# Routing weights of a mixture-of-experts block: transposed by TensorE, or by their transfer to device memory

## The chip, the cores and the metric

The kernel runs on one core of a Trainium2 chip. The metric is device time in microseconds; before the change it is 2189.81 us (median of three runs, 2189.57 to 2190.14).

## The reference

Input `x` is 16 batches x 512 tokens x 128 features, all float32. A first stage adds gated attention (16 heads of 64, causal). The second stage, where the change is, computes for each token:

```python
h = layernorm(x) * (1 + cb) + sb                      # cb, sb, gb per batch
logits = h @ Wr + br                                  # 8 experts
masked = where(logits >= second_largest, logits, -inf)
weights = softmax(masked)                             # two of eight are non-zero
hid = gelu(h @ W1[e] + b1[e])                         # 128 -> 512, each expert
y = sum_e (hid @ W2[e] + b2[e]) * weights[:, e]       # 512 -> 128
x = x + gb * y
```

All eight experts are computed for all tokens.

## The kernel before, in words

Each engine runs its own instruction list, written out by hand, and the lists meet at semaphores. There are two stages, one after the other: attention for all 16 batches (until about 1420 us of the span), then the experts for all 16 batches. Only the second stage is touched.

In the second stage the 512 tokens of a batch lie along the free axis and the features (or hidden units) on the 128 partitions. The stage runs batch by batch (`b`, the first and last written out, the 14 between in a loop), and in each batch over the experts `e` = 0 to 7. A product of high precision is made of three products of rounded operands (high x high, low x high, high x low). The order in one expert step is:

- TensorE: `first_layer(b, e)`, 4 chunks of 128 hidden units, 12 matmuls (L869 to L871); then `second_layer(b, e-1)`, 12 matmuls (L882 to L884) into one of two PSUM banks. TensorE is one expert ahead of itself, so that the activation of `e` lies beside the second layer of `e-1`. Extra work: at e = 1 `sum_T(b-1)` (four transposes, L891), at e = 3 `norm_T` (L845), at e = 4 `router_logits` (L851), at e = 6 `weights_T` (L858), all but the first for batch b+1.
- ScalarE (ACT): four GELU evacuations (L1005) and the rounded high part of chunks 0 and 1 (L1013). Extra: at e = 4 `h_evac`, at e = 5 the exponential, at e = 7 `weights_out` (L985) and `round_h` (L978), at e = 1 `gate_sum` (L992).
- VectorE (DVE): `rest_chunk` for four chunks: the low part (L1124), for chunks 2 and 3 also the high part (L1122); then `weigh_expert(b, e-1)` (L1137). Extra: statistics at e = 1 (L1066, L1069), `finish` (L1146), normalised rows at e = 2 (L1074), `choose` at e = 4 (L1084 to L1091), `weights` at e = 5 (L1096 to L1103), `rest_h` at e = 7 (L1079, in front of chunk 1).
- GpSimd (POOL): `add_expert` (L943) adds each weighted expert to `acc`.
- SP issues the transfers: `store(b-1)`, then `lay_weights(b+1)`.

The weights' way before the change: DVE writes `w_now` as [token, tile, expert] in a buffer of 128 columns per tile whose other columns POOL cleared once (L955). TensorE transposes its four 128x128 tiles into PSUM bank 6 (L858), ACT copies the 8 rows of 512 to `w_T` (L985), SP stores them in device memory as rows of 2 KB (L1198) and, when they have landed, loads each expert's row back to all 128 partitions (`w_rows`, L1204). The row of expert `e` may be overwritten once the batch before has been weighed with it (`y_weighted`). `weigh_expert` computes (y + b2) * weight with `w_rows[:, e, :]` read contiguously.

TensorE waits for `hid_lo_ok` of each chunk before the second layer, for `r_lo` (from `rest_h`) before the first layer of a new batch, and for the weighing two experts back before it reuses a PSUM bank.

Of the kernel before, what the change touches and what calls it, by code (L numbers as in the profile page):

```python
# [7 lines left out]
ALU = mybir.AluOpType  # L8
ACT = mybir.ActivationFunctionType
AX = mybir.AxisListType  # L10
ds = bass.ds
# [27 lines left out]
def adaln_moe_kernel(nc, resid, W_Q, W_K, W_V, W_out, b_out, W1, b1, W2, b2, Wr, br, c_in, wmod, out):  # L39
# [10 lines left out]
    with ExitStack() as ctx:  # L50
# [3 lines left out]
        def sem(name):  # L54
            return ctx.enter_context(nc.semaphore(name))
# [709 lines left out]
        with ExitStack() as pb:  # L765
            def sbb(name, shape, dt=F32):
                return sb(name, shape, dt, pb)
# [17 lines left out]
            shifted = sbb("shifted", [P, NT, E])  # L785
            expd = sbb("expd", [P, NT, E])
            kept = sbb("kept", [P, NT, E])
            w_now = sbb("w_now", [P, NT, P])
            w_sum = sbb("w_sum", [P, NT])
            w_rsum = sbb("w_rsum", [P, NT])  # L790
            w_T = sbb("w_T", [E, S])


            w_rows = sbb("w_rows", [P, E, S])
# [4 lines left out]
            y_result = sbb("y_result", [P, NT, D])  # L799
            y_banks = [banks[:, 4, :], banks[:, 5, :]]  # L800

            hT_bank, wT_bank, out_bank = banks[:, 6, :], banks[:, 6, :], banks[:, 6, :]
            logit_bank = banks[:, 7, 0:NT * E]

            def tile_of(x, b, t):
# [11 lines left out]
            def expert(b, e):  # L817
# [1 line left out]
                return E * b + e  # L819

            load_w = [[sem(f"load_w{layer}_{e}") for e in range(E)] for layer in (1, 2)]
            w_hi_ok, w_split_ok, w_now_clear = sem("w_hi_ok"), sem("w_split_ok"), sem("w_now_clear")
            r_stat, r_mv, r_eps, r_rstd, r_xn = (sem(f"r_{n}") for n in ("stat", "mv", "eps", "rstd", "xn"))
            r_T_ps, r_full, r_hi, r_lo = (sem(f"r_{n}") for n in ("T_ps", "full", "hi", "lo"))
            r_logit_ps, r_shift, r_exp, r_w, r_wT_ps, r_wT = (
                sem(f"r_{n}") for n in ("logit_ps", "shift", "exp", "w", "wT_ps", "wT"))
            w_written = sem("w_written")
            w_laid = [sem(f"w_laid_{e}") for e in range(E)]
            r_chain = sem("r_chain")
# [9 lines left out]
            with nc.Block() as block:  # L839
                @block.tensor  # L840
                def _(pe):
# [6 lines left out]
                    def router_logits(b):  # L848
# [2 lines left out]
                            mm = pe.matmul(logit_bank[:, t * E:(t + 1) * E], hf[:, t * P:(t + 1) * P],  # L851
                                           wr_sb[:, :], start=True, stop=True)
                        mm.then_inc(r_logit_ps, 1)

                    def weights_T(b):
                        pe.wait_ge(r_w, b + 1)
                        for t in range(NT):
                            mm = pe.transpose(wT_bank[:, t * P:(t + 1) * P], w_now[:, t, :], ident[:, :])  # L858
                        mm.then_inc(r_wT_ps, 1)

                    def first_layer(b, e, begin):
                        if e == 0:
# [32 lines left out]
                    def body(b, first, last):  # L895
                        for e in range(E):
                            if first:
                                pe.wait_ge(w_split_ok, e + 1)
                            first_layer(b, e, first and e == 0)
                            if e == 0 and first:  # L900
                                weights_T(0)
                            if first and e > 0:
                                pe.wait_ge(w_split_ok, E + e)
                            if e > 0:
                                second_layer(b, e - 1, first and e < 3)
                            elif not first:
                                second_layer(b - 1, E - 1, False)
                            if e == 1 and not first:
                                sum_T(b - 1)
                            if not last and e == 3:  # L910
                                norm_T(b + 1)
                            if not last and e == 4:
                                router_logits(b + 1)
                            if not last and e == 6:
                                weights_T(b + 1)
                            if first and e == E - 1:
                                pe.wait_ge(w_split_ok, 2 * E)

# [6 lines left out]
                @block.gpsimd  # L925
                def _(pool):
                    def inv_std(b):

                        wait_alone(pool, r_mv, NT * b + NT)
                        pool.tensor_scalar(var_eps[:, :], meanvar[:, :, 1], EPS, 1.0, ALU.add, ALU.mult).then_inc(r_eps, 1)  # L930
                        pool.wait_ge(r_eps, b + 1)
                        pool.tensor_tensor(rstd[:, :], var_eps[:, :], neg_half[:, :], ALU.pow).then_inc(r_rstd, 1)

                    def summed(b, e):

                        return (E - 1) * b + e

                    def add_expert(b, e):
                        wait_alone(pool, y_weighted, expert(b, e) + 1)
                        if e > 1:  # L940

                            wait_alone(pool, y_summed, summed(b, e - 1))
                        pool.tensor_tensor(acc[:, :], acc[:, :], y_w[:, :], ALU.add).then_inc(y_summed, 1)  # L943

                    def body(b, first, last):
                        if not first:
                            add_expert(b - 1, E - 1)
                        if not last:
                            inv_std(b + 1)
                        for e in range(1, E - 1):  # L950
                            add_expert(b, e)

                    inv_std(0)

                    pool.memset(w_now[:, :, :], 0.0).then_inc(w_now_clear, 1)  # L955
                    batches(pool, body)
                    add_expert(B - 1, E - 1)

                @block.scalar
                def _(act):  # L960
# [12 lines left out]
                    def round_h(b):  # L973
# [2 lines left out]

                            act.wait_ge(hid_ps, HC * expert(b, 0))
                        act.activation(h2_hi[:, :], hf[:, :], ACT.Copy).then_inc(r_hi, 1)  # L978

                    def weights_out(b):  # L980
                        act.wait_ge(r_wT_ps, b + 1)
                        if not isinstance(b, int) or b > 0:

                            act.wait_ge(w_written, 16 * b)
                        act.activation(w_T[:, :], wT_bank[0:E, :], ACT.Copy).then_inc(r_wT, 1)  # L985

                    def gate_sum(b):
                        act.wait_ge(y_summed, (E - 1) * (b + 1))
# [26 lines left out]
                    def body(b, first, last):  # L1015
                        for e in range(E):
                            young = first and e < 2
                            if first and e == 1:
                                for other in range(HC):
                                    round_w(2, other)  # L1020

                                act.wait_ge(w_split_ok, E + HC)
                            if first and HC <= e + 2 < E:
                                round_w(2, e + 2)
                            hidden_chunk(b, e, 0, young)
                            if e == 0 and first:
                                weights_out(0)
                            if e == 4 and not last:
                                h_evac(b + 1)
                            if e == 7 and not last:  # L1030
                                weights_out(b + 1)
                            hidden_chunk(b, e, 1, young)
                            round_chunk(b, e, 0, young)
                            hidden_chunk(b, e, 2, young)
                            if e == 7 and not last:
                                round_h(b + 1)
                            round_chunk(b, e, 1, young)
                            hidden_chunk(b, e, 3, young)
                            if e == 1 and not first:
                                gate_sum(b - 1)  # L1040
                            if e == 5 and not last:
                                logit_exp(b + 1)
# [10 lines left out]
                def _(dve):  # L1053
# [40 lines left out]
                    def weights(b):  # L1094
# [2 lines left out]
                        link(b, dve.tensor_reduce(w_sum[:, :], kept[:, :, :], AX.X, ALU.add))  # L1097
                        link(b, dve.reciprocal(w_rsum[:, :], w_sum[:, :]))
                        rsum = w_rsum[:, :].unsqueeze(2).broadcast_to([P, NT, E])
                        if isinstance(b, int) and b == 0:  # L1100

                            dve.wait_ge(w_now_clear, 1)
                        dve.tensor_tensor(w_now[:, :, 0:E], kept[:, :, :], rsum, ALU.mult).then_inc(r_w, 1)  # L1103
                        assert links[0] == CHAIN

                    def split_w(i, layer, e):
# [5 lines left out]
                    def rest_chunk(b, e, c, young):  # L1112
# [3 lines left out]
                        else:  # L1116
# [7 lines left out]
                        dve.tensor_tensor(hid_lo[:, e % 2, c, :], full, hi.bitcast(F32), ALU.subtract)\  # L1124
                            .then_inc(hid_lo_ok, 1)

                    def weigh_expert(b, e, begin):

                        dve.wait_ge(y_ps, expert(b, e) + 1)
# [4 lines left out]
                        if e > 1:  # L1134

                            dve.wait_ge(y_summed, (E - 1) * b + e - 1)
                        dve.scalar_tensor_tensor(out=acc[:, :] if e == 0 else y_w[:, :], in0=y_banks[e % 2],  # L1137
                                                 scalar=b2_cols[:, e:e + 1], in1=w_rows[:, e, :],
                                                 op0=ALU.add, op1=ALU.mult).then_inc(y_weighted, 1)

                    def finish(b, begin):
# [44 lines left out]
                def _(sp):  # L1186
# [7 lines left out]
                                     W2[e].rearrange("(c p) d -> p c d", p=P)).then_inc(load_w[1][e], 16)  # L1194

                    def lay_weights(b, first):
                        sp.wait_ge(r_wT, b + 1)
                        sp.dma_start(w_kept[ds(b, 1)].rearrange("b e s -> e (b s)"), w_T[:, :]).then_inc(w_written, 16)  # L1198
                        sp.wait_ge(w_written, 16 * (b + 1))
                        for e in range(E):  # L1200
                            if not first:
# [45 lines left out]
```

## Time and profile before

| | |
|---|---|
| median of three runs | 2189.81 us |
| the profiled execution | 2190.27 us, its span 2188.5 us |
| TensorE (PE) matmuls | 2047.3 us busy, 94% of the span |
| VectorE (DVE) | 1700.8 us, 78% |
| ScalarE (ACT) | 1531.4 us, 70% |
| GpSimd (POOL) | 722.2 us, 33% |
| granted TensorE clock | 0.994 of full speed |

"Busy" is the time in which an engine has an instruction under way; matmuls overlap one another, so the start-to-start distance of matmuls is the better clock of TensorE. Names such as `banks` are all PSUM banks; `b_cols` stands for `b1_cols` or `b2_cols`, `w_hi` for the high part of either weight.

### The profile page before, as it was taken

Reading aid. Unit: us, or ns where it says so; the run is one execution under the profiler, and the core shown is the slowest. Engines: PE = TensorE matmul, PEld = TensorE weight load, DVE = VectorE, ACT = ScalarE, POOL = GpSimd, SP = SyncE. Lnnn points to the kernel's source line nnn. Section 1 sums busy time; section 2 is a strip of 40 time slices with the busy share of each in tenths; the row PEclk is TensorE's granted clock in tenths of the full one; section 3 lists DMA queues with packets and bytes.
Section 4 is the critical chain, followed back from the end, with each engine's and each line's share of the span. In section 5 each row is a group of like instructions: output and inputs, shape, how many; then the busy total and the mean of one; then the engine's idle time right before and its main releaser. Section 6 shows DMA issues by size and latency. Waiting matters only on the chain. (4 is left out here: it accounts for less than half of the span.)

```text
span 2188.5 us, 45861 instructions
## 1 busy us (share of the span) xinstructions
PE 2047.3 (94%) x12751; PEld 1550.8 (71%) x12751; DVE 1700.8 (78%) x4517; ACT 1531.4 (70%) x3749; POOL 722.2 (33%) x1215
## 2 busy tenths in 40 slices
PE   5999999999999999999999999879999999999998
PEld 3676666666666666667666667568888888888887
DVE  5877767777777677777777777579999888898887
ACT  4777667667677676676677767567776777676775
POOL 2334334333333333333343434212222222222222
PEclk9999999999999999999999999989999999999999
DMA  3000000000000000000000000031211112111111
GB/s 109 16 1 1 0 1 1 0 0 1 0 1 0 1 1 0 1 1 0 1 0 0 1 0 1 1 116 47 75 50 47 43 43 69 56 48 43 43 47 45
DMA packets 41996, 49.99 MB, mean 23 GB/s; under 512 B 3176, under 2 KB 23712, under 8 KB 41888
## 3 DMA queue, kind: packets, MB, share of 16 engines
q1 hardware_dynamic: 41632, 48.41, 7.0%
q0 software_dynamic: 256, 0.53, 0.1%
q14 instruction: 88, 0.72, 0.1%
q8 instruction: 20, 0.33, 0.1%
HBM read 44.47 MB, written 4.46 MB: 22 GB/s over the span
## 5 line engine op out<-in xcount | busy, mean ns | idle before, releaser
L340 POOL TENSOR_SCALAR probs<-probs,rdenom 128x512 f32<-128x512 f32 (+3 forms) x1024 | 522.4, 532 | 840.6 <-DVE rdenom L694 840.6
L564 ACT ACTIVATE probs<-probs,neg_max 128x512 f32<-128x512 f32 (+3 forms) x1024 | 562.8, 553 | 287.2 <-DVE neg_max L685 287.2
L685 DVE CUSTOM_DVE_ANT_0 probs<-banks,mask_w 128x512 f32<-128x512 f32 (+3 forms) x1024 | 441.0, 485 | 66.7 <-PE banks L398 53.5
L1005 ACT ACTIVATE hidden<-banks,b_cols 128x512 f32<-128x512 f32 x512 | 348.4, 685 | 198.5 <-PE banks L871 172.9
L1124 DVE TENSOR_TENSOR hid_lo<-hidden,hid_hi 128x512 fp32r<-128x512 f32 x512 | 386.7, 763 | 67.5 <-ACT hid_hi L1013 55.2
L427 PE MATMUL banks<-ident,probs 128*128 128x128 f32 x2560 | 392.2, 280 | 46.4 <-DVE z_lo L698 34.0
L427 PEld LDWEIGHTS banks<-ident,probs 128*128 128x128 f32 x2560 | 289.7, 141 | 154.0 <-DVE probs_T L674 50.7
L943 POOL TENSOR_TENSOR acc<-acc,y_w 128x512 f32<-128x512 f32 x112 | 155.1, 1385 | 489.5 <-DVE y_w L1137 489.5
L439 PE MATMUL banks<-probs_T,v_sb 128*64 128x512 f32 (+3 forms) x2048 | 303.9, 439 | 1.6 <-DVE probs_T L674 1.6
L674 DVE COPY probs_T<-banks 128x512 f32<-128x512 f32 x384 | 261.7, 681 | 55.4 <-PE banks L427 54.6
L439 PEld LDWEIGHTS banks<-probs_T,v_sb 128*64 128x64 f32 x2048 | 136.0, 137 | 152.4 <-issue 124.2
L398 PE MATMUL banks<-k_hi,q_hi 64*128 64x512 f32 (+3 forms) x1024 | 189.1, 361 | 46.1 <-DVE k_lo L662 31.9
L698 DVE TENSOR_TENSOR z_lo<-banks,z_hi 128x512 fp32r<-128x512 f32 x128 | 88.5, 692 | 160.1 <-ACT z_hi L576 160.1
L869 PE MATMUL banks<-h_hi,w_hi 128*128 128x512 f32 x512 | 207.2, 405 | 3.8 <-DVE w_lo L1110 2.6
L882 PE MATMUL banks<-hid_hi,w_hi 128*128 128x512 f32 x512 | 199.6, 390 | 1.9 <-DVE w_lo L1110 1.9
L871 PE MATMUL banks<-h_lo,w_hi 128*128 128x512 f32 x512 | 200.9, 392 | 0.0
L870 PE MATMUL banks<-h_hi,w_lo 128*128 128x512 f32 x512 | 200.6, 392 | 0.0
L884 PE MATMUL banks<-hid_lo,w_hi 128*128 128x512 f32 x512 | 199.6, 390 | 0.0
L883 PE MATMUL banks<-hid_hi,w_lo 128*128 128x512 f32 x512 | 199.4, 390 | 0.0
L564 ACT ACTIVATION_READ_ACCUMULATOR probs<-probs,neg_max 128x1 f32 x1024 | 194.6, 190 | 0.0
L398 PEld LDWEIGHTS banks<-k_hi,q_hi 64*128 64x128 f32 x1024 | 99.1, 184 | 105.3 <-issue 81.8
L398 PE MATMUL banks<-k_hi,q_lo 64*128 64x512 f32 (+3 forms) x1024 | 168.7, 320 | 0.0
(138 smaller groups left out, 3506.2 us busy)
## 6 DMA issues: line engine op xcount, KB each, us to landing
w_rows<-w_kept SPq DMA_DIRECT2D x128, 256.0 KB, 3.9
x_all<-in_L_attn_resid_dram SPq DMA_DIRECT2D x16, 256.0 KB, 2.6
out_dram<-y_result SPq DMA_DIRECT2D x16, 256.0 KB, 2.3
w_raw<-in_L_ffn_W_dram SPq DMA_DIRECT2D x12, 256.0 KB, 4.0
hidden<-in_L_ffn_W_dram SPq DMA_DIRECT2D x4, 256.0 KB, 6.3
v_sb<-in_L_attn_W_Q_dram SPq DMA_DIRECT2D x1, 512.0 KB, 6.0
v_sb<-in_L_attn_W_K_dram SPq DMA_DIRECT2D x1, 512.0 KB, 8.1
v_sb<-in_L_attn_W_V_dram SPq DMA_DIRECT2D x1, 512.0 KB, 11.2
```

The lines of the kernel that those rows point to most:

```text
L340: pool.tensor_scalar(part, part, rdenom[:, p % 2, 4 * h + r:4 * h + r + 1], 1.0, ALU.mult, ALU.mult)\
L398: mm = pe.matmul(s_banks[S_BANK[u] + h][:, at:at + n], q[own, p % 2, rows], k[own, p % 2, 0:n], start=start, stop=stop)
L427: mm = pe.transpose(T_BANK[u][:, at:at + P], probs[:, p % 2, h, src:src + P], ident[:, :])
L439: mm = pe.matmul(z_bank[h * DH:(h + 1) * DH, c * P:S], v_sb[:, c, hc:hc + DH], probs_T[:, h, KEY_AT[c]:KEY_AT[c] + n], start=(c == 0), sto ...
L564: act.activation(part, part, ACT.Exp, bias=neg_max[:, p % 2, col:col + 1], scale=-1.0, accum_out=denom[:, p % 2, col:col + 1]).then_inc(p_ ...
L674: dve.tensor_copy(dst, src).then_inc(t_dve, 1)
L685: dve.tensor_tensor_reduce(out=probs[:, p % 2, h, at:at + n], in0=s_banks[S_BANK[u] + h][:, col:col + n], in1=mask_w[:, 512 - n:512], scal ...
L869: pe.matmul(banks[:, c, :], w1_hi[:, e, cols], h2_hi[:, :], start=True, stop=False)
L870: pe.matmul(banks[:, c, :], w1_lo[:, e, cols], h2_hi[:, :], start=False, stop=False)
L871: pe.matmul(banks[:, c, :], w1_hi[:, e, cols], h2_lo[:, :], start=False, stop=True)\
L1005: act.activation(hidden[:, e % 2, c, :], banks[:, c, :], ACT.Gelu, bias=b1_cols[:, e * HC + c:e * HC + c + 1]).then_inc(hid, 1)
L1124: dve.tensor_tensor(hid_lo[:, e % 2, c, :], full, hi.bitcast(F32), ALU.subtract)\
```

## The change

`w_now` becomes [token, expert, tile] (32 values per token). SP stores it as it is: for each token `p` of a tile and each expert the four tiles' values lie side by side, 16 bytes, and go to position `4 p` of the expert's row in device memory. There are 128 x 8 = 1024 such runs in the 16 KB. The TensorE transposes, the ACT copy, `w_T` and POOL's clearing go. The rows that come back are in the order (token, tile), and `weigh_expert` reads them with a step of four values (16 bytes) so that they meet y in the order (tile, token). DVE now waits for the store of the batch before (`w_written`) ahead of writing `w_now`.

```diff
-            w_now = sbb("w_now", [P, NT, P])
+            w_now = sbb("w_now", [P, E, NT])
-            w_T = sbb("w_T", [E, S])
@@ TensorE
-                    def weights_T(b):
-                        pe.wait_ge(r_w, b + 1)
-                        for t in range(NT):
-                            mm = pe.transpose(wT_bank[:, t * P:(t + 1) * P], w_now[:, t, :], ident[:, :])
-                        mm.then_inc(r_wT_ps, 1)
-                            if e == 0 and first:
-                                weights_T(0)
-                            if not last and e == 6:
-                                weights_T(b + 1)
@@ POOL
-                    pool.memset(w_now[:, :, :], 0.0).then_inc(w_now_clear, 1)
@@ ACT
-                    def weights_out(b): ...
-                        act.activation(w_T[:, :], wT_bank[0:E, :], ACT.Copy).then_inc(r_wT, 1)
-                            if e == 0 and first:
-                                weights_out(0)
-                            if e == 7 and not last:
-                                weights_out(b + 1)
@@ DVE
-                        if isinstance(b, int) and b == 0:
-                            dve.wait_ge(w_now_clear, 1)
-                        dve.tensor_tensor(w_now[:, :, 0:E], kept[:, :, :], rsum, ALU.mult).then_inc(r_w, 1)
+                        if not isinstance(b, int) or b > 0:
+                            wait_alone(dve, w_written, 16 * b)
+                        dve.tensor_tensor(w_now[:, :, :].rearrange("p e t -> p t e"), kept[:, :, :], rsum, ALU.mult).then_inc(r_w, 1)
+                    def by_tile(a):
+                        return a[:, :].rearrange("d (t p) -> d t p", t=NT)
-                        dve.scalar_tensor_tensor(out=acc[:, :] if e == 0 else y_w[:, :], in0=y_banks[e % 2],
-                                                 scalar=b2_cols[:, e:e + 1], in1=w_rows[:, e, :],
+                        dve.scalar_tensor_tensor(out=by_tile(acc if e == 0 else y_w),
+                                                 in0=y_banks[e % 2].rearrange("d (t p) -> d t p", t=NT),
+                                                 scalar=b2_cols[:, e:e + 1],
+                                                 in1=w_rows[:, e, :].rearrange("d (p t) -> d t p", t=NT),
                                                  op0=ALU.add, op1=ALU.mult).then_inc(y_weighted, 1)
@@ SP
-                        sp.wait_ge(r_wT, b + 1)
-                        sp.dma_start(w_kept[ds(b, 1)].rearrange("b e s -> e (b s)"), w_T[:, :]).then_inc(w_written, 16)
+                        sp.wait_ge(r_w, b + 1)
+                            sp.dma_start(w_kept[ds(b, 1)].rearrange("b e (p t) -> p (b e) t", t=NT), w_now[:, :, :])\
+                                .then_inc(w_written, 16)
```

## Rows read from the trace of the kernel before

**Rows 1.** Busy time by stretch: length, PE, PEld, DVE, ACT, POOL, clock, DMA share, GB/s.
```profile
1701.70:1747.95 46.25, 46.14 (x214) 38.07 (x213) 41.35 (x82) 33.35 (x56) 10.92 (x9) 1.00 0.16 51
```
**Rows 2.** Timeline of PE in one batch: start, length, operation, count.
```profile
1705.69 0.39 PE L869 MATMUL banks<-h_hi,w_hi 128*128 128x512 f32 x1
...
1711.14 0.60 PE L858 MATMUL banks<-ident,w_now 128*128 128x128 f32 x4
1711.50 0.48 PE L869 MATMUL banks<-h_hi,w_hi 128*128 128x512 f32 x1
...
1714.33 0.39 PE L882 MATMUL banks<-hid_hi,w_hi 128*128 128x512 f32 x1
...
1717.05 0.40 PE L869 MATMUL banks<-h_hi,w_hi 128*128 128x512 f32 x1
```
**Rows 3.** Groups by line, 1520 to 2110 us: busy us, mean ns, idle before.
```profile
L1122 DVE CAST hid_hi<-hidden 128x512 fp32r<-128x512 f32 x205 | 85.9, 419 | 0.0
L1137 DVE SCALAR_TENSOR_TENSOR y_w<-banks,b_cols,w_rows 128x512 f32<-128x512 f32 x89 | 66.3, 745 | 0.0
L985 ACT ACTIVATE w_T<-banks 8x512 f32<-8x512 f32 x13 | 7.4, 571 | 0.0
```
**Rows 4.** Groups by line, 60 to 180 us (attention), one operation at two widths.
```profile
L685 DVE CUSTOM_DVE_ANT_0 probs<-banks,mask_w 128x512 f32<-128x512 f32 x24 | 15.6, 687 | 3.8 <-PE banks L398 3.7
L685 DVE CUSTOM_DVE_ANT_0 probs<-banks,mask_w 128x128 f32<-128x128 f32 x24 | 6.8, 284 | 0.0
```
**Rows 5.** Timeline of DVE in one batch; in brackets idle before, and releaser.
```profile
1708.56 0.84 DVE L1103 TENSOR_TENSOR w_now<-kept,w_rsum 128x32 f32<-128x32 f32 x1
...
1710.45 0.69 DVE L1124 TENSOR_TENSOR hid_lo<-hidden,hid_hi 128x512 fp32r<-128x512 f32 x1 [0.40 <-ACT hid_hi L1013]
...
1713.18 0.75 DVE L1137 SCALAR_TENSOR_TENSOR y_w<-banks,b_cols,w_rows 128x512 f32<-128x512 f32 x1
1714.76 1.35 DVE L1124 TENSOR_TENSOR hid_lo<-hidden,hid_hi 128x512 fp32r<-128x512 f32 x1 [0.83 <-ACT hid_hi L1013]
1716.03 0.68 DVE L1079 TENSOR_TENSOR h_lo<-hf,h_hi 128x512 fp32r<-128x512 f32 x1
...
1721.04 1.36 DVE L1124 TENSOR_TENSOR hid_lo<-hidden,hid_hi 128x512 fp32r<-128x512 f32 x1 [0.34 <-ACT hid_hi L1013]
...
1725.38 0.69 DVE L1124 TENSOR_TENSOR hid_lo<-hidden,hid_hi 128x512 fp32r<-128x512 f32 x1 [0.19 <-ACT hid_hi L1013]
1726.48 1.29 DVE L1124 TENSOR_TENSOR hid_lo<-hidden,hid_hi 128x512 fp32r<-128x512 f32 x1 [0.41 <-ACT hid_hi L1013]
...
1729.82 0.74 DVE L1137 SCALAR_TENSOR_TENSOR acc<-banks,b_cols,w_rows 128x512 f32<-128x512 f32 x1
...
1743.45 1.79 DVE L1124 TENSOR_TENSOR hid_lo<-hidden,hid_hi 128x512 fp32r<-128x512 f32 x2 [1.05 <-ACT hid_hi L1013]
```
**Rows 6.** Timeline of POOL in the same batch.
```profile
1708.05 1.29 POOL L943 TENSOR_TENSOR acc<-acc,y_w 128x512 f32<-128x512 f32 x1 [4.70 <-DVE y_w L1137]
1714.26 1.29 POOL L943 TENSOR_TENSOR acc<-acc,y_w 128x512 f32<-128x512 f32 x1 [4.92 <-DVE y_w L1137]
1720.36 1.48 POOL L943 TENSOR_TENSOR acc<-acc,y_w 128x512 f32<-128x512 f32 x1 [4.81 <-DVE y_w L1137]
1725.46 1.76 POOL L943 TENSOR_TENSOR acc<-acc,y_w 128x512 f32<-128x512 f32 x1 [3.61 <-DVE y_w L1137]
...
1742.67 1.29 POOL L943 TENSOR_TENSOR acc<-acc,y_w 128x512 f32<-128x512 f32 x1 [4.87 <-DVE y_w L1137]
```
**Rows 7.** Timeline of SP's DMA issues in the same batch.
```profile
1713.81 0.32 SPq L1198 DMA_DIRECT2D w_kept<-w_T  x1
1715.47 10.22 SPq L1204 DMA_DIRECT2D w_rows<-w_kept  x8
```
**Rows 8.** The page on DMA: a queue's packets, MB, share of 16 engines; issues, KB, us to landing.
```profile
q1 hardware_dynamic: 41632, 48.41, 7.0%
...
w_rows<-w_kept SPq DMA_DIRECT2D x128, 256.0 KB, 3.9
```

More of the change, by code:

```diff
@@ L800, in adaln_moe_kernel @@
             y_banks = [banks[:, 4, :], banks[:, 5, :]]
-            hT_bank, wT_bank, out_bank = banks[:, 6, :], banks[:, 6, :], banks[:, 6, :]
+            hT_bank, out_bank = banks[:, 6, :], banks[:, 6, :]
             logit_bank = banks[:, 7, 0:NT * E]
@@ L821, in adaln_moe_kernel @@
             load_w = [[sem(f"load_w{layer}_{e}") for e in range(E)] for layer in (1, 2)]
-            w_hi_ok, w_split_ok, w_now_clear = sem("w_hi_ok"), sem("w_split_ok"), sem("w_now_clear")
+            w_hi_ok, w_split_ok = sem("w_hi_ok"), sem("w_split_ok")
             r_stat, r_mv, r_eps, r_rstd, r_xn = (sem(f"r_{n}") for n in ("stat", "mv", "eps", "rstd", "xn"))
             r_T_ps, r_full, r_hi, r_lo = (sem(f"r_{n}") for n in ("T_ps", "full", "hi", "lo"))
-            r_logit_ps, r_shift, r_exp, r_w, r_wT_ps, r_wT = (
-                sem(f"r_{n}") for n in ("logit_ps", "shift", "exp", "w", "wT_ps", "wT"))
+            r_logit_ps, r_shift, r_exp, r_w = (
+                sem(f"r_{n}") for n in ("logit_ps", "shift", "exp", "w"))
             w_written = sem("w_written")
@@ L978, in round_h @@
                         act.activation(h2_hi[:, :], hf[:, :], ACT.Copy).then_inc(r_hi, 1)
[L980 to L984, printed above, removed]
-                        act.activation(w_T[:, :], wT_bank[0:E, :], ACT.Copy).then_inc(r_wT, 1)
                     def gate_sum(b):
@@ L1196, in lay_weights @@
                     def lay_weights(b, first):
-                        sp.wait_ge(r_wT, b + 1)
-                        sp.dma_start(w_kept[ds(b, 1)].rearrange("b e s -> e (b s)"), w_T[:, :]).then_inc(w_written, 16)
+                        sp.wait_ge(r_w, b + 1)
+                        with nc.allow_non_contiguous_dma("expert rows of the routing weights"):
+                            sp.dma_start(w_kept[ds(b, 1)].rearrange("b e (p t) -> p (b e) t", t=NT), w_now[:, :, :])\
+                                .then_inc(w_written, 16)
                         sp.wait_ge(w_written, 16 * (b + 1))
```

## The prediction

> **What bounds the kernel now.** I read the busy time by stretch first. One period of the expert stage is 46.25 us; TensorE is busy in 46.14 of them, DVE in 41.35, ACT in 33.35, POOL in 10.92 [rows 1]. So TensorE sets the pace, and the reader should see how near DVE is behind it. TensorE's timeline gives the unit: from 1705.69 to 1711.14 lie 24 matmul starts, 0.227 us each [rows 2]. 192 of them are 43.6 us; transposes, logits and a short wait make up the rest.
>
> DVE's 41.35 us hide something. The timelines of DVE and POOL, laid beside each other, show that the two exclude each other when DVE reads two operands from the local memory: the product written to hid_lo lasts 0.69 us at 1710.45, but 1.35 at 1714.76, 1.36 at 1721.04 and 1.29 at 1726.48, each time until POOL's addition is through [rows 5, 6]. The other way about, POOL's addition takes 1.29 us where DVE leaves it alone and 1.76 at 1725.46, where a DVE product had just begun. Even the small write of w_now lasts 0.84 us, up to the end of the addition that began at 1708.05 [rows 5, 6]. POOL takes part of DVE's time, then, about 1.15 us per addition (1.76 less the 0.61 that the product at 1725.38 still had to run).
>
> **How much can DVE take on?** Its idle pieces, all with ACT as releaser, are 0.40, 0.83, 0.34, 0.19, 0.41 and 1.05 us [rows 5]. A DVE that is late would not wait for ACT, but it would still have to let POOL through. The 0.34 and 0.41 lie inside POOL's turns (1720.36 with 1.48, 1725.46 with 1.76 [rows 6]) and can't be had. Of the 0.83 some 0.55 can, since the addition of 1714.26 would start after the product in place of before it; of the 1.05 some 0.36, by the same working with the addition of 1742.67 [rows 6]. With 0.40 and 0.19 that is 1.5 us. DVE needs 46.25 - 1.5 = 44.75 us per period, against TensorE's 46.25.
>
> **The change, part by part.**
>
> *TensorE's four transposes go.* From 1711.14 to 1714.33 stand the transposes and 12 matmuls: 3.19 us, less 12 x 0.227 = 2.72, is 0.47 us [rows 2]. TensorE's period falls to 45.78. There are 15 such places in running batches: 7.0 us if nothing else is late. What is late next is `rest_h`, which ends at 1716.03 + 0.68 = 1716.71 [rows 5], while the first matmul of the next batch, at 1717.05 [rows 2], would come at 1716.58. The ACT copy that also goes (0.57 us [rows 3]) stands ahead of the rounding that `rest_h` waits for, so it moves up too; it loses at most 0.13 us per batch, 2 us in all. In the first batch the transposes and the copy lie between short waits: between 0 and 1.0 us, I take 0.5.
>
> *The ACT copy and POOL's clearing* cost nothing today: ACT has 12.9 idle us per period [rows 1], and POOL clears once, before the stage runs. Gain counted above, none beside it.
>
> *w_now.* The write keeps its size (32 values), and its wait for POOL. The new wait for `w_written` concerns a transfer issued a batch earlier, long done. `wait_alone` adds an empty instruction on DVE: between 0 and 0.3 us (the idle between linked small operations is some 0.1); I take 0.1 us. Behind it is queued hid_lo of expert 6; its last chunk is ready when the weighing at 1713.18 begins [rows 5] and wanted by the tenth matmul after 1714.33 [rows 2], at 1716.4: 3 us to spare.
>
> *The store to device memory.* It is issued at about 1709.5 instead of 1713.81 [rows 5, 7], 4.3 us earlier, since it no longer waits for TensorE and ACT. SP's queue holds nothing between: the output store of the batch before is done by then. Today it is through in 1715.47 - 1713.81 = 1.66 us [rows 7]. With 1024 runs of 16 bytes, 64 for each of 16 engines, I take the mean packet: 7.0% of 16 x 2188.5 us over 41632 packets is 59 ns [rows 8], so 3.8 us, and 5 us with the way there and back. From above: a row load brings 8 runs per engine in 3.9 us [rows 8], 0.49 us each with all latency in it, or 31 us for 64. The first row is wanted by the weighing at 1729.82 [rows 5] and takes 3.9 us itself: 1729.82 - 1709.5 - 3.9 leaves 16.4 us. At 5 us it is hidden, and SP's eight loads (10.22 us, the last ones held by the weighings [rows 7]) shift with nobody waiting. Cost: 0; it decides only above some 0.23 us per run.
> The Trainium skill speaks against this part (DMA: Bandwidth & Descriptors, "Rules for kernel authors"): a transposition by rearranging a plain transfer is given there as 19 times slower than the hardware's. No row here has such a transfer; 19 times the 1.66 us would be 32 us, late by 15 us per batch.
>
> *Weighing with a step of 16 bytes.* It is the large term. Today it takes 0.745 us [rows 3], eight times per batch. No row shows a DVE operand read with a large step, so I bound it. From below: no change; arithmetic and element count are the same. From above: each value of the stepped operand costs a second turn. A turn is (687 - 284) ns / 384 = 1.05 ns [rows 4], so 512 of them are +0.54 us, and the weighing would take 1.28. The nearest rows say that DVE's pace is one of fetching, not of arithmetic: 512 values from the local memory to the local memory pass in 0.42 us, while the weighing, with an operand from PSUM, takes 0.75 [rows 3]. An operand whose neighbours lie four values apart gives one useful value per fetch, so I take the upper end, +0.54 us, and keep zero as the other. (A penalty for POOL comes on top nowhere: its addition still starts after the weighing.)
> The Trainium skill has a rule on it (SBUF — State Buffer, the note on 16-byte cachelines in its port section): full bandwidth needs at least two hits per line of 16 bytes, and each new line costs. Every value here is in a new line. It names no price, and no row here tests it; by it the weighing slows, without it the sum is the rival below.
>
> **The sum.** DVE's need becomes 44.75 + 0.1 + 8 x 0.54 = 49.1 us per period, above TensorE's 45.78. DVE becomes the bound: +2.9 us per batch over today's 46.25, in 14 batches +40 us. TensorE starts with the 3 us that hid_lo is ahead of it to use up, once: -3. The first batch has seven weighings on a DVE that the splitting of weights keeps full: +4, less 0.5. The last batch has no routing for a successor, so DVE is over TensorE by some 0.25 us per expert: +2. The last two weighings stand on the closing chain: +1. Together 40 - 3 + 3.5 + 2 + 1 = 43.5 us. The profiled execution took 2190.27 us, 0.46 above the median of the three; 2190.3 + 43.5 = 2234 us.
>
> **The rivals.**
>
> *A, the step costs nothing.* Then DVE needs 44.85, stays under 45.78, and the whole 0.47 per batch is had: 2190.3 - 7.0 - 0.5 = 2182.8, up to 2185 with `rest_h` late. This is the other side, and it turns on one price. It decides while the weighing is below 0.745 + (45.78 - 44.85)/8 = 0.86 us; at 0.745 + (46.25 - 44.85)/8 = 0.92 us the two balance and the time is as before. For it: DVE takes one value per 1.05 ns from any source in these rows, with room for a second read; against it, the argument of fetches.
>
> *B, half the price* (+0.27 us, weighing 1.01): need 44.85 + 2.16 = 47.0, +0.75 us in 14 batches is 10.5, less the lead of 3, plus 3 for the ends: about 2201. Nothing in the rows speaks for a half, beside that the other operand, from PSUM, may hide part.
>
> *C, the store is late*, above 0.23 us per run. At the upper bound of 31 us each batch would wait 15 us for its first row: 15 x 15 = 220 us more, by DVE standing at L1137 with a DMA as releaser. Against it: 59 ns per packet, and a margin of four.
>
> *D, it doesn't do what it says*: the transposes' 0.47 us go, but `rest_h` gives none of it and ACT's order takes it back; 2190 without the step's price. Little speaks for it, since the wait there is 0.13 us at most.
>
> **How the numbers follow.** Forecast (full price) 0.52, its own range 2222 to 2246 (2.9 us per batch with 0.8 either way, for my reading of what POOL leaves DVE). A 0.31, B 0.11, C 0.04, D 0.02. A change of under 0.2% (4.4 us) can't be told from none here. Faster by more: A, most of it, 0.30. Same: D, a small part of A and B, 0.05. Slower: 0.65. Between the forecast and A lies nearly all of the chance, so the range runs from 2181 to 2244; it leaves out C and the top of the forecast.
>
> **What would show it.** L858 and L985 gone, TensorE's step behind the last L884 of expert 5 at 0.23 us: the saving. L1137 at 1.28 us mean in place of 0.745: the price; at 0.75 A holds, and I am wrong at that step. With the price, DVE is busy in 98% of a period of some 49 us without waits for ACT, and TensorE idles ahead of L882 with L1124 as releaser. The first row load issued about 5 us after the store, at 1714 to 1715 on today's scale. If L1137 is at 1.28 and the period still below 47, my reading of POOL's share of DVE's time is wrong.

## The result: 0.9% slower, and the profile after

| | before | after |
|---|---|---|
| median of six runs | 2190.57 us | 2210.33 us |
| ratio, 95% interval | | 1.0088, 1.0075 to 1.0101 |
| span of the profiled execution | 2188.5 us | 2208.2 us |

The change costs 19.8 us. The forecast was +43.5 us: the right sign and, as the runs below show, the right mechanism (VectorE's stepped read makes VectorE the bound), but more than twice the size.

A period is the distance of two `logits` additions in DVE's timeline, one batch of work. One period of the changed kernel by busy time, with the columns of [rows 1]:

```profile
1755.36:1802.84 47.48, 45.96 (x209) 37.57 (x209) 45.37 (x83) 33.04 (x55) 10.95 (x9) 1.00 0.17 50
```

The period went from 46.25 to 47.48 us. TensorE is busy in 45.96 of them and idle in 1.5; DVE rose from 41.35 to 45.37. The groups by line between 1540 and 2110 us (busy us, mean ns of one, idle before) show what grew; [rows 3] has the same operations before:

```profile
L1116 DVE SCALAR_TENSOR_TENSOR y_w<-banks,b_cols,w_rows 128x512 f32<-128x512 f32 x84 | 94.9, 1130 | 0.0
L1055 DVE TENSOR_TENSOR h_lo<-hf,h_hi 128x512 fp32r<-128x512 f32 x12 | 21.4, 1781 | 0.0
L1098 DVE CAST hid_hi<-hidden 128x512 fp32r<-128x512 f32 x192 | 80.2, 418 | 0.0
```

The weighing takes 1.13 us in place of 0.745. The write of 0.42 us (L1098) is unchanged. The product `h_lo` (0.68 us at 1716.03 in [rows 5]) now lasts 1.78 in the running batches: it comes while POOL's addition is under way.

The timeline of TensorE has idle time in front of two instructions in this period. Both are waits that a late DVE makes; neither stands ahead of the second layer (L875 to L877 here), where the prediction looked for them:

```profile
1770.27 0.49 PE L862 MATMUL banks<-h_hi,w_hi 128*128 128x512 f32 x1 [0.87 <-DVE h_lo L1055]
...
1782.11 0.66 PE L884 MATMUL banks<-ident,acc_gated 128*128 128x128 f32 x4 [0.65 <-ACT acc_gated L972]
```

DVE's timeline from 1766.69 to 1782.11 has no idle piece. The same stretch in [rows 5] had 0.83, 0.34, 0.19 and 0.41 us:

```profile
1766.69 1.13 DVE L1116 SCALAR_TENSOR_TENSOR y_w<-banks,b_cols,w_rows 128x512 f32<-128x512 f32 x1
1767.74 0.68 DVE L1100 TENSOR_TENSOR hid_lo<-hidden,hid_hi 128x512 fp32r<-128x512 f32 x1
1768.34 1.77 DVE L1055 TENSOR_TENSOR h_lo<-hf,h_hi 128x512 fp32r<-128x512 f32 x1
...
1772.76 1.12 DVE L1116 SCALAR_TENSOR_TENSOR y_w<-banks,b_cols,w_rows 128x512 f32<-128x512 f32 x1
1773.81 2.38 DVE L1100 TENSOR_TENSOR hid_lo<-hidden,hid_hi 128x512 fp32r<-128x512 f32 x2
```

Two products of `hid_lo` last 2.38 us where a pair alone takes 1.28: 1.10 us is POOL's turn.

The new store is not late. SP's timeline (start, length of issuing, line), against [rows 7]:

```profile
1763.64 0.41 SPq L1180 DMA_DIRECT2D w_kept<-w_now  x1
1767.20 12.67 SPq L1187 DMA_DIRECT2D w_rows<-w_kept  x8
```

From the store to the first row load are 3.56 us, against 1.66, and no DVE wait has a DMA as releaser.

### The profile page after: what moved, and what is told of

It is laid out like the page before. It is cut to its first block and busy times, and to the rows that moved or that the text cites. A ratio compares the mean times of both kernels' runs of the same rounds, so it can differ in the third digit from the quotient of the medians.

```text
span 2208.2 us, 45716 instructions
## 1 busy us (share of the span) xinstructions
PE 2043.8 (93%) x12687; PEld 1542.9 (70%) x12687; DVE 1763.8 (80%) x4517; ACT 1526.3 (69%) x3733; POOL 727.3 (33%) x1214
## 5 line engine op out<-in xcount | busy, mean ns | idle before, releaser
L1100 DVE TENSOR_TENSOR hid_lo<-hidden,hid_hi 128x512 fp32r<-128x512 f32 x512 | 391.1, 778 | 23.7 <-ACT hid_hi L993 12.1
L875 PE MATMUL banks<-hid_hi,w_hi 128*128 128x512 f32 x512 | 199.6, 390 | 1.1 <-DVE w_lo L1086 1.1
L877 PE MATMUL banks<-hid_lo,w_hi 128*128 128x512 f32 x512 | 199.2, 389 | 0.0
```

## The experiments

Fourteen kernels beside the changed one ran. Times are medians, and each ratio is to the kernel before on the same chip; four kernels, named below, ran once each. Kernels that read the weights in a wrong order, or leave work out, serve only to price one part.

**The step alone, taken away and put in alone.** The first kernel is the changed one with

```diff
-  in1=w_rows[:, e, :].rearrange("d (p t) -> d t p", t=NT)
+  in1=w_rows[:, e, :].rearrange("d (t p) -> d t p", t=NT)
```

> The changed kernel, but the weighing reads each expert's row contiguously (so tokens meet other tokens' weights); the 16-byte store and everything else stay. Theory (the step is the whole loss): the weighing is back at 0.745 us, the period falls from 47.48 to 45.8 us, the first batch keeps its 3.1 us gain: about 2180 us. Rival (the turned store or DVE's new wait carries part of the loss): above 2190 us with the weighing at 0.745.

Measured: 2180.41 us, ratio to before 0.9953 (0.9936 to 0.9970); weighing 0.745 us. Its period by busy time:

```profile
1743.03:1788.83 45.80, 45.70 (x210) 37.56 (x209) 41.36 (x83) 33.03 (x55) 11.07 (x9) 1.00 0.17 52
```

45.80 us, 0.45 us below the kernel before: the transposes' removal gives that much per batch, and the store costs nothing. The loss is the step. The second kernel adds only the stepped read to the kernel before:

> The kernel before, with only the weighing's stepped read added (transposes, copy and store as before; weights meet wrong tokens). Theory (the period is a loop that goes through DVE from expert 3 to the last weighing and through TensorE only from the closing transposes to expert 3): the transposes at expert 6 lie off that loop, the period is 47.5 as in the changed kernel, and only the first batch's 3 us are missing: about 2213 us. Rival (TensorE's 0.47 us add to DVE's price): period 47.95, about 2220 us.

Measured: 2211.04 us, ratio 1.0095 (1.0078 to 1.0112); weighing 1.128 us. Its period:

```profile
1757.05:1804.51 47.46, 46.39 (x213) 37.93 (x213) 45.34 (x83) 33.34 (x56) 10.97 (x9) 1.00 0.15 50
```

TensorE has 0.43 us more work here than in the changed kernel, and the period is the same. Once DVE is the bound, what the change took off TensorE buys nothing in a running batch. The first batch's 3 us, which the expectation added, show only as 0.7 us in the medians, less than the intervals can tell from nothing.

**What POOL takes of DVE.** In the changed kernel, step kept:

```diff
-  pool.tensor_tensor(acc[:, :], acc[:, :], y_w[:, :], ALU.add)
+  pool.tensor_tensor(acc[:, 0:8], acc[:, 0:8], y_w[:, 0:8], ALU.add)
```

> The changed kernel, stepped read kept, but POOL adds only 8 of the 512 columns of each weighted expert (the rest of the sum is left out). Theory (POOL's additions take about 1.1 us each of DVE's time, and that makes the DVE's price bind): DVE gets 5 to 6 us per batch back, TensorE binds again at 45.4 to 45.8: about 2178 us, with the weighing still at 1.13 us. Rival (DVE's own durations are the whole bound): 47.5 less only the stretch of the closing addition, about 1.3 us, once per batch at most: 2190 us or above.

Measured: 2171.68 us, ratio 0.9919 (0.9902 to 0.9936), with the weighing still at 1.12 us. One period by busy time, then DVE's group of `hid_lo` and of the write of `w_now`:

```profile
1738.09:1783.54 45.45, 45.45 (x210) 37.72 (x209) 40.34 (x83) 32.90 (x55) 2.96 (x9) 1.00 0.17 52
```

```profile
L1100 DVE TENSOR_TENSOR hid_lo<-hidden,hid_hi 128x512 fp32r<-128x512 f32 x401 | 273.4, 690 | 50.7 <-ACT hid_hi L993 41.2 <-DVE chosen L1067 2.6
L1079 DVE TENSOR_TENSOR w_now<-kept,w_rsum 128x32 f32<-128x32 f32 x13 | 2.8, 217 | 2.2 <-DVE w_rsum L1074 2.2
```

DVE's busy time falls by 5.0 us per period, though no DVE instruction was changed: `hid_lo` is at its bare 0.69 us and `w_now` at 0.22 in place of 0.79. TensorE has no idle piece left. So the stepped read alone would fit beside TensorE; step and POOL's turns together don't. The time fell 6 us below the theory's. The period is 0.35 us shorter than that of the first kernel, 4.9 us over 14 batches. There TensorE's loads for the closing transposes waited for the gated sum, here that wait is gone. I take it for the source, and no run isolates it. The loads in the first kernel, then in this one:

```profile
L884 PEld LDWEIGHTS banks<-ident,acc_gated 128*128 128x128 f32 x52 | 5.4, 141 | 6.9 <-ACT acc_gated L972 6.9
```

```profile
L884 PEld LDWEIGHTS banks<-ident,acc_gated 128*128 128x128 f32 x48 | 6.0, 142 | 1.6
```

**Which weighings count.** The contiguous read for experts 0 to 2 only, and for 3 to 5 only:

```diff
-  in1=w_rows[:, e, :].rearrange("d (p t) -> d t p", t=NT)
+  in1=by_row(e) if e < 3 else w_rows[:, e, :].rearrange("d (p t) -> d t p", t=NT)      # first kernel
+  in1=by_row(e) if 3 <= e <= 5 else w_rows[:, e, :].rearrange("d (p t) -> d t p", t=NT)  # second
```

> The changed kernel with the contiguous read for experts 0, 1 and 2 only (their tokens meet wrong weights), the stepped one for 3 to 7. Theory (the period is a loop: DVE from expert 3's low parts to the last weighing, then POOL, ACT and the closing transposes, then TensorE and ACT back to DVE; the weighings of experts 0 to 2 lie beside TensorE's part): only the first batch gains, about 2209 us, period 47.5. Rival (the sum of DVE's work is the bound, wherever it stands): 3 x 0.384 = 1.15 us less per batch, about 2193 us.

> The same for experts 3, 4 and 5: contiguous there, stepped for 0, 1, 2, 6 and 7. Theory of the loop: all three lie on DVE's part, 1.15 us less per batch, period 46.3, about 2192 us. Rival (DVE's sum): the same 2193 us; it is the pair with the kernel before this one that tells them apart, 17 us apart by the loop and equal by the sum.

Measured: 2202.44 us (ratio 1.0062, 1.0044 to 1.0080) and 2192.87 us (1.0013, 1.0003 to 1.0022). The commonest periods are 46.86 and 46.36 us, with longer ones of up to 47.78 (one of 49.38) and 47.06 between them that were not explained. The pair are 9.6 us apart, so neither theory holds in full. In the commonest periods three equal savings on DVE are worth 1.12 us per batch at experts 3 to 5 and 0.62 at 0 to 2 (as means over 14 periods 1.04 and 0.42): where they stand matters, against the plain sum, but those beside TensorE's part are not free, against the loop as I had drawn it. DVE's timeline of the first kernel shows by what the saving gets in, against the changed kernel's:

```profile
1746.05 0.75 DVE L1119 SCALAR_TENSOR_TENSOR y_w<-banks,b_cols,w_rows 128x512 f32<-128x512 f32 x1
1747.82 1.79 DVE L1100 TENSOR_TENSOR hid_lo<-hidden,hid_hi 128x512 fp32r<-128x512 f32 x2 [1.03 <-ACT hid_hi L993]
```

```profile
1796.32 1.13 DVE L1116 SCALAR_TENSOR_TENSOR y_w<-banks,b_cols,w_rows 128x512 f32<-128x512 f32 x1
1797.37 0.68 DVE L1100 TENSOR_TENSOR hid_lo<-hidden,hid_hi 128x512 fp32r<-128x512 f32 x1
1798.46 1.30 DVE L1100 TENSOR_TENSOR hid_lo<-hidden,hid_hi 128x512 fp32r<-128x512 f32 x1 [0.40 <-ACT hid_hi L993]
```

After the weighing of expert 2 DVE waits for ACT in both, so time saved before it is partly lost in the wait (1.03 us against 0.40). But the weighing also starts POOL's addition, which then stands in front of the next product, and an earlier weighing gets that turn over earlier. I take this place for the source of the 0.62 us; these lines don't give the number, and no run isolates it.

**What a step costs, and on which side.** Four forms of the changed kernel ran once each: a step of two, a step of eight, then the row contiguous with y read from PSUM by a step of four, then both read contiguously and the result written by a step of four. Their times have no interval; the reading is the length of the weighing, which each kernel does 128 times.

```diff
+  in1=w_rows[:, e, :].rearrange("d (p t) -> d t p", t=2)      # or t=8
+  in0=y_banks[e % 2].rearrange("d (p t) -> d t p", t=NT)      # PSUM
+  out=(acc if e == 0 else y_w)[:, :].rearrange("d (p t) -> d t p", t=NT)   # result
```

> The changed kernel with a step of two values (8 bytes) in the weighing's read in place of four (tokens meet wrong weights). Theory (cost per 16-byte line: two values of each line are met one after the other): the weighing is at 0.745 us, time about 2180. Rival (any step costs): between 0.85 and 1.13 us.

> The changed kernel with a step of eight values (32 bytes). Theory (each value in a line of its own, at 16 bytes already): the weighing stays at 1.13 us, time about 2210. Rival (the price grows with the distance): above 1.2 us.

> The changed kernel with the row read contiguously and y read from PSUM with a step of four values (features meet wrong tokens). Theory (each source has its own fetch, and PSUM's is as dear or dearer): 1.13 us or more. Rival (the step costs only on the local memory's side): 0.745 us.

> The changed kernel with both sources contiguous and the result written with a step of four values (the sum is then in the wrong token order). Theory (a write needs no second turn): 0.745 us, time about 2180. Rival (a write to a new line costs as a read does): 1.13 us.

Measured, with the group of the weighing between 1540 and 2110 us of each, in this order (busy us, mean ns of one, idle before): 2179.34 us,

```profile
L1116 DVE SCALAR_TENSOR_TENSOR y_w<-banks,b_cols,w_rows 128x512 f32<-128x512 f32 x87 | 64.8, 745 | 0.0
```

2222.42 us,

```profile
L1116 DVE SCALAR_TENSOR_TENSOR y_w<-banks,b_cols,w_rows 128x512 f32<-128x512 f32 x82 | 99.1, 1208 | 0.0
```

2178.46 us,

```profile
L1119 DVE SCALAR_TENSOR_TENSOR y_w<-banks,b_cols,w_rows 128x512 f32<-128x512 f32 x87 | 64.8, 745 | 0.0
```

2203.48 us:

```profile
L1119 DVE SCALAR_TENSOR_TENSOR y_w<-banks,b_cols,w_rows 128x512 f32<-128x512 f32 x84 | 96.0, 1143 | 0.0
```

A step of 8 bytes is free, 16 bytes cost 0.38 us, 32 bytes 0.46 (single weighings there last between 1.13 and 1.27 us, which was not explained). That agrees with the rule of the Trainium skill quoted in the prediction (SBUF — State Buffer, two hits per line of 16 bytes) where the cost begins. The same note also says that one may stride for free up to 4 fp32; as a step of four values, 16 bytes, that is not so here, and the measurement decides. The rise from 16 to 32 bytes is not in it. From PSUM a step is free, against my theory; a stepped write costs as much as a stepped read, against it too.

**Turning the order with the store alone.** The contiguous weighing, and

```diff
-  w_kept[ds(b, 1)].rearrange("b e (p t) -> p (b e) t", t=NT)
+  w_kept[ds(b, 1)].rearrange("b e (t p) -> p (b e) t", t=NT)
```

> The changed kernel with the turning done wholly by the store: single values of 4 bytes, 4096 runs, go to their place in tile order, and the weighing reads contiguously. Theory: the 16-byte store took 3.56 us to the next issue against 1.66 before, so 30 ns per run and engine; 256 runs are 7.7 + 1.7 = 9.4 us, under the 16.4 us that are free: 2180 us, faster than both kernels. Rival (each run costs the 59 ns of the mean packet or more): 17 us or more, the first weighing of each batch late by 1 us or more: 2195 us or above.

Measured: 2186.82 us, ratio 0.9984 (0.9975 to 0.9992). The trace gives for the transfers from `w_now` "DMA to landing us min/median/max: 14.1/15.6/16.3". With 4096 runs, 256 per engine, and 1.6 us of way there and back, that looks like 55 ns a run, the rival's rate. It just fits into the 16.4 us of a running batch, and in the first batch it doesn't:

```profile
1456.08 0.75 DVE L1119 SCALAR_TENSOR_TENSOR acc<-banks,b_cols,w_rows 128x512 f32<-128x512 f32 x1 [6.41 <-DMA w_rows<-w_kept]
```

6.4 us are the difference from 2180.41. So I cut the store in four, each followed by its two row loads:

> The store of single 4-byte values, cut into four transfers of two experts each; the two rows that a transfer feeds are loaded before the next is issued. Weighing contiguous, all of the sum computed. The undivided store landed after 15.6 us, 55 ns per run and engine; a quarter is 64 runs, 3.5 + 1.6 = 5 us. Theory (the undivided store lost only where the first batch waited 6.4 us for row 0): that wait goes, about 2180.5 us, below the kernel before by 9 us. Rival (a share of the 6.4 us is the transfers' traffic or SP's order in every batch): 2184 us or above.

Measured: 2214.22 us, ratio 1.0116 (1.0098 to 1.0134): a miss by 34 us. The waits of DVE and SP, in total us, times, and the longest:

```profile
DVE w_now L1080 <- DMA w_kept<-w_now: 46.4, 15, 6.7
```

```profile
SPq L87 <- DMA w_kept<-w_now: 631.6, 64, 11.7
```

SP waits 631.6 / 64 = 9.9 us for each quarter, where a quarter of the whole store's 15.6 us is 3.9. Four of them in a row last into the next batch, and DVE waits to write `w_now`.

The traces show where the time goes. In the first batch SP issues a quarter at 1438.04 and goes on at 1446.04. By busy time (the last two columns are the DMA share and GB/s) nothing moves in the second half of that wait:

```profile
1438.00:1442.00 4.00, 2.34 (x11) 1.60 (x10) 3.93 (x8) 2.73 (x6) 0.00 (x0) 1.00 0.64 142
1442.00:1446.00 4.00, 4.00 (x18) 3.21 (x18) 2.15 (x4) 2.30 (x5) 0.00 (x0) 1.00 0.00 0
```

The undivided store, issued at 1711.50 with the first row load at 1727.35, has the same:

```profile
1711.50:1719.30 7.80, 7.80 (x36) 6.37 (x35) 6.88 (x12) 5.51 (x10) 1.50 (x1) 1.00 0.45 2
1719.30:1727.35 8.05, 8.05 (x37) 6.67 (x36) 7.58 (x12) 5.97 (x11) 1.83 (x2) 1.00 0.00 0
```

After the last recorded packet of single values 8 us pass in the whole store and 4 us or more in that quarter; in the changed kernel, with runs of 16 bytes, it is 1.90 us (1765.30 to 1767.20). So the 55 ns per run is no rate of the packets: half of the 15.6 us lies behind them, and each quarter has such a piece of its own. What passes in that piece stays open.

**The order turned where it is cheap.** The weighing reads y from PSUM in the order (token, tile), everything else contiguously; the sum is turned back once per batch, by ACT's gate in the first kernel, by the closing transposes in the second:

```diff
-  in0=y_banks[e % 2].rearrange("d (t p) -> d t p", t=NT)
+  in0=y_banks[e % 2].rearrange("d (t p) -> d p t", t=NT)
-  in1=w_rows[:, e, :].rearrange("d (p t) -> d t p", t=NT)
+  in1=w_rows[:, e, :].rearrange("d (p t) -> d p t", t=NT)
# second kernel
-  pe.transpose(out_bank[:, t * P:(t + 1) * P], acc_gated[:, t * P:(t + 1) * P],
+  pe.transpose(out_bank[:, t * P:(t + 1) * P], acc_gated[:, :].rearrange("d (p t) -> d t p", t=NT)[:, t, :],
```

> The changed kernel, all of it computed, with the order turned elsewhere: the weighing reads y from PSUM in the order (token, tile), a step of 128 values, and the row and the result contiguously; ACT turns the sum back once per batch when it applies the gate (a stepped read of 512 values). Theory (the step costs nothing on the PSUM side, as a step of four did, and is paid once per batch, on the closing chain): weighing 0.745, period 45.8 plus at most ACT's 0.4: 2180 to 2187 us. Rival (a step of 512 bytes in PSUM is not free as one of 16 was): weighing above 1.0 us, 2205 us or more.

> As the kernel before this one, but the closing transposes read the gated sum with a step of four values and ACT reads contiguously. Theory (TensorE's load of four 128-column tiles is off its pace, so a slower read costs 0.2 us per batch or nothing): 2180 to 2184 us, the fastest. Rival (TensorE pays per value as DVE does, 4 x 128 x 0.75 ns = 0.4 us per batch): 2187 us, equal to ACT's way.

Measured: 2188.29 us, ratio 0.9994 (0.9984 to 1.0003), not told from the kernel before and just above the expected 2180 to 2187; and 2182.57 us, ratio 0.9969 (0.9956 to 0.9981). The weighing is at 0.745 us in both, with a step of 512 bytes in PSUM. The groups that pay, ACT's gate in the first and TensorE's loads in the second:

```profile
L972 ACT ACTIVATE acc_gated<-acc,gate_cols 128x512 f32<-128x512 f32 x12 | 14.7, 1227 | 4.9 <-POOL acc L932 4.9
```

```profile
L884 PEld LDWEIGHTS banks<-ident,acc_gated 128*128 128x128 f32 x52 | 7.3, 211 | 6.9 <-ACT acc_gated L972 6.9
```

ACT's gate took 0.72 us in the kernel before and takes 1.23, all on the closing chain: the period is 46.30 us, 0.50 above the contiguous kernel's 45.80. A load of weights by TensorE takes 0.21 us in place of 0.14, for four loads per batch; the period is 45.93. The second kernel computes the whole reference and beats both: 7.3 us below the kernel before.

**The first batch.** In the kernel before, only ACT's copy of the first batch is moved:

```diff
                             hidden_chunk(b, e, 0, young)
-                            if e == 0 and first:
-                                weights_out(0)
...
                             hidden_chunk(b, e, 3, young)
+                            if e == 0 and first:
+                                weights_out(0)
```

> The kernel before, with one move: in the first batch ACT's copy of the turned weights stands after the fourth hidden chunk in place of after the first. Theory (the changed kernel's 3.1 us head start in the first batch came from that copy, which held ACT for 3.4 us until TensorE had transposed): about 2187 us. Rival (it came from the transposes' own time on TensorE): 2189.5 us or more.

Measured: 2187.18 us, ratio 0.9988 (0.9979 to 0.9997). ACT's timeline of the kernel before and of this one, with the idle time in front:

```profile
1438.60 0.59 ACT L985 ACTIVATE w_T<-banks 8x512 f32<-8x512 f32 x1 [3.44 <-PE banks L858]
```

```profile
1438.68 0.57 ACT L985 ACTIVATE w_T<-banks 8x512 f32<-8x512 f32 x1
```

The copy stood in ACT's queue and held three hidden chunks for 3.44 us, until TensorE had transposed. Behind the chunks the wait is gone: the first weighing begins at 1449.32, with 1452.31 in the kernel before and 1449.25 in the changed one.

## Why the prediction was off in size

Point by point, by its own steps:

- *TensorE bound before, DVE 1.5 us behind.* Right. With the step taken away the period is 45.80 us, forecast 45.78; the 0.47 us of the transposes came out as 0.45.
- *POOL's turns are part of what DVE must carry.* Right, and shown by the small addition: 5.0 us of DVE's busy time per period. Counted by busy time alone, DVE's 41.35 us plus the measured 3.1 for the step are below 45.8, and the change would have looked like a gain.
- *DVE's wait on `w_written`, ACT's copy in running batches, the store.* All hidden, as said. The store has 3.3 us to landing as its median, forecast 5. The figure of the Trainium skill, 19 times, compares a rearranging transfer with the hardware's own transposition, which no run here has. I set it against the 1.66 us of a store of plain rows, which is not what it says. Against those rows, runs of 16 bytes take 3.56 us to the next issue, and single values 15.85.
- *The price of the step, +0.54 us.* This is the term that failed. I took a whole second turn for each value; measured are 0.384 us, 0.75 ns per value instead of 1.05. The turn came from an attention operation [rows 4], with the claim that DVE takes one value per 1.05 ns from any source; the cast of 0.42 us in [rows 3] is 0.82 ns per value, start-up included, and contradicts it. That a second turn is what happens is not shown either; the runs show only where the price begins and its size. Eight times 0.154 us are 1.23 us per batch, 17 us over 14 batches: most of the 23.7 us by which the forecast was too high. I had kept zero and 0.27 as rivals and gave the space between 0.27 and 0.54 no case of its own.
- *DVE's need, 44.85 us without the price.* Too high by 0.44: 44.85 + 8 x 0.384 = 47.92, measured 47.48, or 6 us over 14 batches. From weighing to weighing, before against after less 0.384, DVE made up 1.8 us of idle time where I allowed 1.5, and its new wait cost nothing where I took 0.1; and it still waits 0.40 us for ACT once per batch, at 1798.46, where I had it never wait. Nor did TensorE wait where I had it: not ahead of the second layer for `hid_lo`, but 0.87 us for `h_lo` and 0.65 for the gated sum. With the pair at experts 0 to 2 and 3 to 5, I read the period as a loop through both engines and not as DVE's sum.
- *The first batch, -0.5 us before its weighings.* Measured -3.1: its first weighing began at 1449.25 instead of 1452.31. I had looked at TensorE's small waits, not at what stood behind ACT's copy.
- *The ends and TensorE's lead of 3 us, used up once.* 14 x 1.23 = 17.2 of the 19.8 us lie in running batches, so the small terms come to +2.6 us together, where +3.5 was forecast. In the profiled executions the changed kernel is 1.5 us ahead at the second `logits` addition, 1.5 behind at the third, 16.6 more behind at the last, and loses 1.7 after it. The first running distance grew by 3.0 us, the whole price of eight steps, and none is shorter by a lead. The first batch's gain was six times what I took. That the sum of these terms is near is luck.

The time lies between the forecast and rival B (half the price, 2201 us), and so does the price, 0.384 us between 0.27 and 0.54. Rival A's price is that of a step of 8 bytes, or of one in PSUM. Rival C's mechanism, a late store, did come, but only with runs of 4 bytes.

## What to carry to other kernels

Before an operand is read in another order, ask on which memory and how often: here the same turning cost 0.38 us at each of 128 weighings from the local memory, nothing from PSUM, and 0.07 us at each of 64 loads on TensorE. Count an engine's room together with what its neighbour takes of it: DVE looked 11% idle and had 4% (1.8 of 46.25 us). A copy that waits for another engine belongs behind the work that doesn't.

## What the runs showed of the hardware

- A DVE operation of 512 float32 values with one operand in PSUM and one in local memory takes 0.745 us; a step in the local operand of 8 bytes adds 0, of 16 bytes 0.38, of 32 bytes 0.46 (one execution each for 8 and 32); a step of 16 bytes in the result adds 0.40; a step of 16 or 512 bytes in the PSUM operand adds 0.
- POOL's additions, seven per batch, cut from 512 values to 8, gave DVE back 5.0 us of busy time; a pair of DVE products with both operands in the local memory lasts 2.38 us with one and 1.28 without.
- ACT's read of 512 values with a step of 16 bytes adds 0.50 us to 0.72, more than DVE's.
- TensorE's load of 128x128 float32 with a step of 16 bytes takes 0.21 us against 0.14.
- A store of 16 KB takes 3.3 us to landing in 1024 runs of 16 bytes and 15.6 us in 4096 runs of 4 bytes; 1024 runs of 4 bytes kept SP waiting for 9.9 us. With runs of 4 bytes a large part of the wait, 8.05 us in one whole store, lies behind the last recorded packet and was not explained.
